# A new call order on every engine, second moments and warm-up matmuls in diagonal blocks, and other PSUM banks for the first steps of a recurrence

## The reference

```python
x = x + conv_ref(gn(x))            # group norm; linear attention with 4 heads; layer norm
t = tokens(x)                      # 16 x 256 tokens of 32 channels
t = t + attn_ref(ln(t))            # causal softmax attention, one head of 32
t = t + ffn_ref(ln(t))

def ffn_ref(x, W, V, gamma, beta):
    Wx = einsum('bti,hi->bth', x, W)
    mean, var = Wx.mean over all 4096 rows, Wx.var over all 4096 rows   # one pair per channel
    Wx = (Wx - mean) * rsqrt(var + 1e-5) * gamma + beta
    def step(yt, wx_t):
        yt = sigmoid(wx_t + yt @ V.T); return yt, yt
    _, ys = scan(step, zeros, Wx over the 256 time steps)
    return ys
```

## Time and profile before

| | |
|---|---|
| median of 3 runs | 94.66 us (94.57 to 96.39) |
| the profiled execution | 94.73 us |
| its span, first to last instruction | 93.0 us |
| PE busy | 80.7 us (87% of the span), 1090 matmul records |
| DVE, ACT, POOL busy | 64.1, 53.9, 41.0 us |
| DMA | 1.89 MB, mean 20 GB/s |

### The profile page before, as it was taken

One profiled execution on the slowest core, in us unless ns is written; L12 is line 12 of the kernel. 1 busy time (PEld: TensorE's weight loads), 2 busy tenths in 40 slices (PEclk: granted clock), 3 DMA queues, 4 the chain that ended last, 5 costly groups with the idle time before them and its releaser, 6 DMA issues.

```text
span 93.0 us, 2823 instructions
## 1 busy us (share of the span) xinstructions
PE 80.7 (87%) x1090; PEld 56.8 (61%) x1090; DVE 64.1 (69%) x174; ACT 53.9 (58%) x163; POOL 41.0 (44%) x79
## 2 busy tenths in 40 slices
PE   5998599989999968979699799999998977888950
PEld 1335286767676647557577567667896835566730
DVE  5868955949759996894694298287459557766670
ACT  5045979475085188563916754952858965656620
POOL 5700387060497969657059733432986020000030
PEclk9999999999999999999999999999999999999996
DMA  1644000000000000000000002010000200000035
GB/s 20 112 73 68 10 0 0 7 0 11 4 7 0 0 7 4 0 7 0 0 7 0 0 0 63 0 56 1 0 7 28 85 0 0 0 0 0 7 96 133
DMA packets 8445, 1.89 MB, mean 20 GB/s; under 512 B 7376, under 2 KB 8432, under 8 KB 8432
## 3 DMA queue, kind: packets, MB, share of 16 engines
q1 hardware_dynamic: 7904, 1.58, 8.2%
q10 hardware_dynamic: 528, 0.13, 0.5%
HBM read 0.66 MB, written 0.52 MB: 13 GB/s over the span
## 4 chain that ended last, share of the span: by engine, by line
PE 58%; DVE 21%; ACT 8%; issue 5%; DMA 3%; POOL 1%; SPq 0%; DVEq 0%; POOLq 0%
PE pair L1734 8%; PE pair L1480 6%; PE pair L1200 3%; ACT warm L855 3%; DVE z L947 3%; PE pair L1330 3%; PE pair L1442 3%; PE pair L1367 3%; DMA x_tok<-in_x_dram 3%; DVE max_b L919 3%; PE pair L1295 3%; DVE max_b L921 3%; PE pair L1419 3%; PE pair L1414 2%; PE pair L1301 2%
## 5 line engine op out<-in xcount | busy, mean ns | idle before, releaser
L653 ACT ACTIVATE eqk<-pair 128x512 f32<-128x512 f32 x16 | 8.7, 598 | 3.9 <-PE pair L1314 3.8
L1149 DVE TENSOR_SCALAR pair<-wxT,bn_sc 128x256 f32<-128x256 f32 x14 | 7.5, 546 | 3.7 <-ACT warm L855 3.0
L1734 PE MATMUL pair<-warm,w_bd 128*128 128x124 f32 (+3 forms) x44 | 7.9, 302 | 2.1 <-DVE pair L1149 0.8
L1200 PE MATMUL pair<-idle_b 128*128 128x512 bf16 x23 | 8.6, 479 | 1.1 <-DVE idle_b L876 1.1
L693 ACT ACTIVATE eqk<-pair 128x384 f32<-128x384 f32 x16 | 6.9, 495 | 3.4 <-PE pair L1461 3.4
L482 POOL TENSOR_TENSOR z<-z 128x512 f32<-128x512 f32 x4 | 5.1, 1267 | 8.3 <-DVE z L947 8.3
L1734 PEld LDWEIGHTS pair<-warm,w_bd 128*128 128x128 f32 x44 | 5.9, 188 | 4.5 <-ACT warm L855 3.2
L855 ACT ACTIVATE warm<-pair 128x124 f32<-128x124 f32 (+2 forms) x20 | 5.1, 276 | 3.7 <-PE pair L1734 3.7
L919 DVE TENSOR_REDUCE max_b<-pair 128x16 bf16<-128x512 f32 x8 | 5.5, 685 | 2.0 <-PE pair L1272 1.9
L568 POOL TENSOR_TENSOR eqk<-warm,ys 128x126 f32<-128x126 f32 x2 | 0.8, 428 | 13.4 <-ACT ys L855 13.4
L1367 PE MATMUL pair<-ctxo,eqk 64*64 64x66 f32 x256 | 5.6, 224 | 0.9 <-DVE z L947 0.5
(11 more groups left out here) (208 smaller groups left out, 208.1 us busy)
## 6 DMA issues: line engine op xcount, KB each, us to landing
x_tok<-in_x_dram SPq DMA_DIRECT2D x8, 64.0 KB, 2.5
eqk<-t SPq DMA_DIRECT2D x8, 64.0 KB, 2.2
out_dram<-out_tok SPq DMA_DIRECT2D x1, 256.0 KB, 2.7
out_dram<-out_tok SPq DMA_DIRECT2D x1, 128.0 KB, 2.3
out_dram<-out_tok ACTq DMA_DIRECT2D x1, 128.0 KB, 2.6
w_raw<-in_L_conv_w_qkv_dram SPq DMA_DIRECT2D x1, 48.0 KB, 2.2
wout_sb<-in_L_conv_w_out_dram SPq DMA_DIRECT2D x1, 16.0 KB, 2.3
brow<-in_L_conv_b_out_dram SPq DMA_DIRECT2D x1, 16.0 KB, 3.1
```

The lines of the kernel that those rows point to most:

```text
L653: act.activation(eqk[:, r, g], bank[g][:], ACT.Exp).then_inc(s_expA, 1)
L1149: dve.tensor_scalar(parts[s][:, :, 0:RPC * CHUNKS].rearrange("p c (r h j) -> p c r h j", r=RPC, h=HALVES), wxT[:].rearrange("p (c r) (h m ...
L1200: pe.matmul(bank[at][:], idle_b[:], idle_b[:, 0:1].broadcast_to([P, 512]), start=True, stop=True)
L1734: pe.matmul(part(c, s), vT_bd, src, start=False, stop=True, skip_group_check=True).then_inc(s_pre[c], 1)
```

## The change

1. **Order.** The lists of PE, ACT, DVE and POOL are written anew, without changing what most functions do. Six `awake` calls fewer stand ahead of the recurrence.
2. **Moments in blocks.** `gram_2` computes only the four diagonal 32 x 32 blocks, each with 32 columns of ones beside it, as four matmuls of 32 output rows for each of the 8 operands. `moments` shrinks from 129 to 33 columns, its mask becomes a copy, and `ffn_moments` is four matmuls of 33 columns.
3. **Warm-up matmuls in blocks.** In steps 1 to 11 the product with `vT_bd` is four matmuls of 32 x 32 weights, one for each diagonal block.
4. **Banks and the start.** `parts` is rotated, so that step 1 uses the pair that is free first. Seed 1 is written one chain at a time, and waits for two `awake` matmuls that stand early; seeds 2 and 3 wait for later ones.

The core of the diff (of the four lists only some lines):

```diff
-        parts = [(pair[0], pair[1], mid_pair)[s % 3] for s in range(STEPS)]
+        parts = [(pair[1], mid_pair, pair[0])[s % 3] for s in range(STEPS)]
...
 # ACT's list
-            sel_out_qk()
             gn(0)
+            wqk_cast()
             gn_cast(0)
-            wqk_cast()
+            wqk_out()
             gn(1)
-            wqk_out()
+            wout_centre()
...
 # DVE
-                dve.tensor_tensor(moments[:], bank[0][:, 0:P + 1], mask_sum[:], ALU.mult).then_inc(s_moments, 1)
+                dve.tensor_copy(moments[:], bank[0][:, 0:C + 1]).then_inc(s_moments, 1)
...
                 if s >= 4:
                     for c in range(CHAINS):
                         dve.wait_ge(s_y[c], s - 2)
+                else:
+                    dve.wait_ge(s_full, s)
+                if s == 1:
+                    for c in range(CHAINS):
+                        dve.tensor_scalar(parts[1][:, c, 0:RPC * CHUNKS].rearrange("p (r h j) -> p r h j", r=RPC, h=HALVES),
+                                          wxT[:, RPC * c:RPC * (c + 1)].rearrange("p r (h m j) -> p m r h j", h=HALVES, m=STRIDE)
+                                          [:, place(1)[0]], bn_sc[:, 4:5], bn_sc[:, 6:7], ALU.mult, ALU.add).then_inc(s_seed, 1)
+                    return
...
-            dve.wait_ge(s_full, 1)
...
 # PE
                 for h in range(HALVES):
-                    ins = pe.matmul(bank[0][:, 0:P + 1], tn2[:, r, h, 0:P], tn2[:, r, h, :],
-                                    start=(r == 0 and h == 0), stop=(r == R - 1 and h == HALVES - 1))
+                    for g in range(G):
+                        ins = pe.matmul(bank[0][C * g:C * (g + 1), 0:2 * C].rearrange("p (k c) -> p k c", k=2),
+                                        tn2[:, r, h, g], tn2[:, r, h, g::G - g],
+                                        start=(r == 0 and h == 0), stop=(r == R - 1 and h == HALVES - 1))
...
-                pe.matmul(bank[1][:, 0:P + 1], w_all[:], moments[:], start=True, stop=True).then_inc(s_bnp, 1)
+                for g in range(G):
+                    at = slice(C * g, C * (g + 1))
+                    ins = pe.matmul(bank[1][at, 0:C + 1], w_all[:, at], moments[:], start=True, stop=True)
+                ins.then_inc(s_bnp, 1)
...
-            for at in (0, 4, 5, 0):
-                awake(at)
+            for at in (4, 5):
+                ins = awake(at)
+            ins.then_inc(s_full, 1)
+            awake(0)
+            pe.wait_ge(s_bnve, 1)
+            awake(1).then_inc(s_full, 1)
             pe.wait_ge(s_wxS, R)
             awake(2)
-            pe.matmul(bank[3][:], idle_b[:], idle_b[:, 0:1].broadcast_to([P, 512]), start=True, stop=True).then_inc(s_full, 1)
+            awake(3).then_inc(s_full, 1)
...
-                    if c == 0:
-                        pe.wait_ge(s_seed, s)
-                    pe.matmul(part(c, s), vT_bd, src, start=False, stop=True,
-                              skip_group_check=True).then_inc(s_pre[c], 1)
+                    if c == 0 or s == 1:
+                        pe.wait_ge(s_seed, c + 1 if s == 1 else s + 1)
+                    if s <= WARM:
+                        for g in range(G):
+                            at = slice(C * g, C * (g + 1))
+                            ins = pe.matmul(part(c, s)[at], vT_bd[at, at], src[at], start=False, stop=True,
+                                            skip_group_check=True)
+                    else:
+                        ins = pe.matmul(part(c, s), vT_bd, src, start=False, stop=True, skip_group_check=True)
+                    ins.then_inc(s_pre[c], 1)
```

More of the change, by code:

```diff
@@ L524, in _ @@
             block_diagonal()
+            gn_cast(1)
+            residual_bias(0)
             output_blocks()
+            residual_bias(1)
             triangles()
-            permutation()
-            ones_columns()
-            gn_cast(1)
-            gn_cast(2)
-            averages()
-            gn_cast(3)
-            block_weights()
-            heads(0)
-            residual_bias(0)
+            residual_bias(2)
+            ones_columns()
+            block_weights()
+            gn_cast(2)
+            gn_cast(3)
+            heads(0)
+            permutation()
             scale_heads(0)
@@ L811, in _ @@
             v1_out(3)
+            values_out(2)
+            square_2(0)
             square_2(1)
-            values_out(2)
             exp_b(3, 0)
@@ L1065, in _ @@
             max_a(2, 0)
+            heads(0, 1)
             max_a(2, 1)
-            heads(0, 1)
+            contexts(1)
             shift_a(2)
-            contexts(1)
             heads(1, 0)
@@ L1116, in _ @@
             gain_2(2)
+            variance(2, 2)
             attend_half(0)
@@ L1197, in awake @@
             def awake(at):
-                pe.matmul(bank[at][:], idle_b[:], idle_b[:, 0:1].broadcast_to([P, 512]), start=True, stop=True)
+                return pe.matmul(bank[at][:], idle_b[:], idle_b[:, 0:1].broadcast_to([P, 512]), start=True, stop=True)
             rep = rep_id[:].rearrange("p g c -> p (g c)")
@@ L1576, in _ @@
             max_a(0, 1)
+            awake(7)
             x_back(0)
@@ L1579, in _ @@
             awake(7)
-            awake(7)
-            awake(7)
             x_in(3)
+            queries(0, 0)
             neg_a(0)
-            queries(0, 0)
             queries(0, 1)
@@ L1588, in _ @@
             keys(0, 1)
+            shifts_a(0, 1)
             x_back(2)
             x_back(3)
-            shifts_a(0, 1)
             projection()
@@ L1596, in _ @@
             grams(0, 1)
-            queries(1, 0)
+            small_rows()
             contexts(0)
             neg_a(1)
-            small_rows()
+            queries(1, 0)
             queries(1, 1)
@@ L1606, in _ @@
             outs(0, 0)
+            small_blocks()
             max_a(2, 0)
-            small_blocks()
+            outs(0, 1)
             max_a(2, 1)
@@ L1611, in _ @@
             grams(1, 1)
-            outs(0, 1)
             queries(2, 0)
+            contexts(1)
             neg_a(2)
-            contexts(1)
+            queries(2, 1)
             keys(2, 0)
             shifts_a(2, 0)
-            queries(2, 1)
             outs(1, 0)
@@ L1622, in _ @@
             max_a(3, 0)
+            outs(1, 1)
             grams(2, 0)
-            outs(1, 1)
+            max_a(3, 1)
             awake(5)
-            max_a(3, 1)
             grams(2, 1)
+            contexts(2)
             queries(3, 0)
-            contexts(2)
-            awake(5)
+            keys(3, 0)
+            queries(3, 1)
             neg_a(3)
-            queries(3, 1)
-            keys(3, 0)
-            keys(3, 1)
             outs(2, 0)
             shifts_a(3, 0)
+            keys(3, 1)
             shifts_a(3, 1)
@@ L1660, in _ @@
             values(0, 1)
-            turn(2)
             scores(1, 0)
@@ L1665, in _ @@
             masks(1, 1)
-            values_back(0)
+            turn(2)
             masks(1, 0)
@@ L1670, in _ @@
             project(2)
+            values_back(0)
             max_b(2, 0)
@@ L1674, in _ @@
             values(1, 1)
+            scores(2, 0)
+            scores(2, 1)
+            masks(2, 1)
             neg_b(2)
-            scores(2, 1)
-            scores(2, 0)
-            masks(2, 1)
+            turn(3)
             masks(2, 0)
-            turn(3)
             shifts_b(2, 0)
             shifts_b(2, 1)
+            project(3)
             values_back(1)
-            project(3)
-            awake(6)
             max_b(3, 0)
```

119 lines of the change are left out of this document (56 added, 63 removed).

## The result

| | before | after |
|---|---|---|
| median, us | 94.61 (94.08 to 96.39, 4 runs) | 91.75 (91.49 to 91.85, 4 runs) |
| profiled execution: time / span, us | 94.73 / 93.0 | 91.85 / 90.1 |
| chain that ended last: PE / DVE / ACT / issue | 58 / 21 / 8 / 5% | 71 / 16 / 7 / 4% |

The change makes the kernel faster: ratio 0.971, 95% interval [0.966, 0.976]; the ratio leaves out one execution of before, 96.39 us, as a slow one. The forecast was 90.7 in a range of 89.0 to 93.4. So the direction and the range held, and of the forecast gain of 4.0 us 2.9 came.

A forecast was written before the change was run, and what follows sets the result against it. No single engine bounds the kernel; time is a walk between engines (PE 58%, DVE 21%), with a latency loop in the steps. 94.73 - 0.85 - 1.75 - 0.65 - 0.77 = 90.7 us, range 89.0 to 93.4.

The forecast's parts named there:

- Head: Start to first exponentials: -0.85 us, from L903 starting 0.37 earlier and 0.48 less waiting for PE work; bounds 0 to -1.0.
- the clock as a rival: Steps: fewer fillers let the clock fall, 0.25 us a step over 14 steps, +3.5, total 95.0; chance 0.07.
- Middle: First exponentials to last `max_b` on PE: reordering at three places removes waits, -1.75 us; bounds +0.5 to -2.8.
- (a): Middle, DVE: `gain(2)` waited 1.11 us for POOL with `heads(3, 0)` and others queued behind; moving them ahead gives 0.8.
- (b): Middle, ACT: the `turn(2)` wait of 2.73 us held the square; `values_out(0)` and `square_z(3)` go first; the rest of 1.75.
- (c): Middle, PE: `values_back` replaces the `awake` at 59.85 and 0.29 idle before the last `max_b`; about 0.5 us.
- The rival of an order that gives nothing: Head and middle: new waits replace each one removed, both stay at 0, total 93.3 us; chance 0.14.
- Moments and start: Before the first step: smaller moments move the first sigmoid -0.2, seed 1 is no longer late; -0.65 us, bounds -0.2 to -0.9.
- Blocks: Steps 1 to 11: four blocks stream together, a pass of 0.43 against 0.50, 0.07 a step, -0.77 us.
- the rival of serial blocks: Steps 1 to 11: the blocks run one after another, +9.9 instead of -0.77, total 101.4 us; chance 0.09.
- the signs named: L903 near 5.95, exponentials 12.2, last `max_b` 58, first step under 0.6 after sigmoid, pass within 0.43, steps 0.78, clock 1.00.
- the three signs of being wrong: A pass over 0.5, PE idle over 3 us in the middle, or `wxT` holding the first sigmoid past 76.

The follow-up runs named there:

- the blocks alone: Kernel before with only the four 32 x 32 blocks in steps 1 to 11 added; 93.92 us, ratio 0.9956.
- after once more: The changed kernel profiled and timed again, unchanged; 91.69 us, ratio 0.967.
- undoing (a): Changed kernel with `gain(2)` back ahead of `heads(3, 0)` in DVE's list; ratio 0.981, from two of seven executions, at 92.53 and 92.70 us.
- undoing (b): Changed kernel with `tnT_out(2)` back ahead of `values_out(0)` and `square_z(3)` in ACT's list; 93.20 us, ratio 0.990.
- the order alone: Changed kernel with full matmuls in the steps, full moments and the old start, leaving new order and rotated banks; 93.29 us, ratio 0.986.
- The run with full moments: Changed kernel with `gram_2`, `moments` and `ffn_moments` of before (128 columns and the mask); 91.56 us.
- the short fillers: Changed kernel with the last two `awake` ahead of step 1 cut from 512 to 128 columns; 90.81 us, ratio 0.960.
- one block: Changed kernel keeping only the first of four blocks in steps 1 to 11, output wrong; total 322.6 us through the step-by-step branch, a step 0.75 us.

## Why the prediction was right, and where its terms were off

**Head: -0.85 forecast, -0.20 in the profiled execution.** The chain was right to L903. What failed is that the durations of before were taken for PE's records, as if dropping two `awake` changed nothing else. In the earlier trace rows three `awake` take 1.49, about 0.5 each, and a later one 0.38; in after's profile they took over 0.6 until 9.68. These durations are not fixed. With the early outcome of the same code the exponentials start at 11.94, 1.06 ahead of before. So against the 13.00 of before the term is about -1.05 or -0.1 to -0.3 by the outcome. Before's head isn't fixed either: in the run with the blocks alone its exponentials started at 12.28, with short records from 3.9 us on. Early against early, as far as two traces tell, it is 11.94 - 12.28 = -0.34. All of it lies behind the first maximum, L919, which starts at 8.08 in that run and at 8.11 in after once more; in the two first profiles it is 8.80 and 8.82. So the 0.37 taken at L903 did not reach the maxima in either comparison; what came is part of the 0.48 taken behind them. The prediction had the clock as a rival, but in the steps and not in the head. The Trainium skill (TensorE: Matmul & The Clock Gate, What's actually happening) says that the start at the lower level varies from run to run of one kernel and is below 1% of a typical span; the traces agree that it varies, and here it is 0.9 of 90, 1%. Whether the two dropped fillers make the late outcome likelier stays open: records stayed long past 9 us in five of ten traces without them, and in none of the four with them (two of before's head, two of after's).

**Middle: -1.75 forecast, -1.48 measured; right in two of its three parts.** Counted from the first exponentials, the first `max_b` of group 1 on DVE (L989) comes 0.93 earlier, the exponentials of group 1 (L693) 1.33, the last `max_b` 1.48. Of the 0.93, 0.17 is there already at the first `max_b` of group 0 (38.56 - 13.00 against 38.19 - 12.80), ahead of place (a). So in sequence (a) gave 0.76 where 0.8 was taken, (b) 0.40 where 0.45 was left, and (c) 0.15 instead of 0.5. The failed size is (c): the `awake` at 59.85 was counted with the 0.29 idle behind it, but the bound there was the cast of `uT` (it ends 0.10 ahead of the last `max_b` in before and 0.11 in after), and `values_back` fills the time. The single moves show that (a) and (b) carry more than their shares when the rest is in place: undoing (a) delayed the next maxima by 1.6 (0.8 to 1.0 in the totals at full clock), undoing (b) cost 2.2. The rival of an order that gives nothing, 93.3, is out by this; the order alone already took 1.64 out of the middle.

**Moments and start: -0.65 forecast, -0.88 measured (0.53 + 0.35).** I had let one more copy of `tn2T` push ACT's last `wxT` copy from 75.36 to 75.7. Counted from the last `max_b`, that copy ended at 14.84 in before and at 73.71 - 58.84 = 14.87 in after, so it did not move:

```profile
72.45 1.26 ACT L582 COPY wxT<-pair 128x256 f32<-128x256 f32 x4
```

The run with full moments shows why. There the copies take 1.69 instead of 1.26 and end at 71.55 + 1.69 - 57.94 = 15.30. So the new order did push them back, by 0.46, and the small moments took 0.43 of that away again: on PE `ffn` of the last groups stands behind `ffn_moments`, and these copies wait for it. This second effect of the moments is what the sum left out. The factors themselves were mis-sized too: with full moments DVE's L1138 starts 15.31 behind the last `max_b`, and in after once more the same instruction (L1137) 14.59, so they come 0.72 earlier and not 0.3 to 0.4. The sigmoid gained 0.63 by the moments alone, and 0.53 in the change as a whole. The start was held by the two last `awake` and not by the seed, though only for about 0.12, as the short fillers showed: the first step begins 0.71 behind the sigmoid's start, over the 0.6 forecast. Their trace gained nothing in its span, probably because the second chain waits for the sigmoid's second half.

**Blocks: -0.77 forecast, about -0.44 measured (0.04 a step).** The mechanism was right, and the rival of serial blocks, 101.4, is out. The pass took 0.46 and not the 0.43 of the earlier trace rows. One block takes 0.41 and each further one 0.02. The row that I priced by has more rows of the array behind each tile, and its loads, 110 ns, are even longer than these, 102; why its eight records are 0.03 shorter no run shows. The Trainium skill (TensorEngine Tiling (Array Packing), Restrictions and Gotchas) says that different row tiles can't access the same bank at once. The traces do not agree for tiles that write to partitions of their own: 0.46 for eight records of one step, against 0.41 for two.

**The clock in the steps** did not fall in any trace of after, but it did in the blocks alone and with one block. So the rival's price (0.25 a step, 0.22 measured) is real. Its reason, fewer fillers, is not shown, since the run with the blocks alone has all those of before; and a lower clock over all 14 steps is not seen in after.

**The total.** The terms miss on both sides: the head by 0.65, the blocks by 0.33 and the middle by 0.27 too little, moments and start by 0.23 too much. Of the signs named, L903 came (5.92); the first exponentials, the last `max_b`, the pass, the step and the distance from the sigmoid to the first step each came later or longer than said. None of the three signs of being wrong came: a pass takes 0.46, PE idles 2.60 us in the middle, and the first sigmoid starts at 73.83.

## What to carry over

When calls are reordered, look for the instruction that waits while others behind it on its engine are ready; here moving one such call back cost 2.2 us in a 90 us kernel and moving the other delayed the next stage by 1.6, while the two gave 0.4 and 0.8 when counted in sequence. Before comparing medians that differ by less than 1 us, cut the traces at the same events: the start of the kernel alone had two outcomes 0.9 us apart with the same code. Small gains ahead of a filler or a seed show only once what stands behind them moves too: the new start was worth 0.35 in the change's sum and 0.89 beside its other parts.

## What the runs showed of the hardware that I had not expected

- Records of PE can be long (an `awake` 0.61 to 0.63 us instead of 0.38) for the first 10 us while the granted clock reads 1.00, and in another execution of the same code from 3.8 us on short.
- In one execution an idle time of 1.7 of 5 us on PE stood ahead of four us at a granted clock of 0.57; in another, with an idle time as long, it stayed at 1.00.
- Four matmuls of 32 x 32 weights in the diagonal blocks of one bank take 0.02 us each beyond the first, and a pass with one block a chain 0.41 us from the first load to the last end, against 0.50 with the full tile. So only 0.09 of 0.50 hangs on the size of the tile.
